# A transformer layer on eight cores: a second weight staging buffer, a reordered attention-output stage, and quantisation work moved between stages

## The reference

```python
# x: (8, 2048, 2048) fp32; Wq, Wk, Wv, Wo: (2048, 2048); w1: (8192, 2048); w2: (2048, 8192)
q, k, v = x @ Wq, x @ Wk, x @ Wv                       # per batch item, 2048 tokens
scores  = swapaxes(q) @ k / sqrt(64)                   # (feature, feature): 2048 x 2048
a       = swapaxes(softmax(scores, -1) @ swapaxes(v))  # contraction over features
x2      = layernorm(x + a @ Wo)
quant(w) = sign(w) * (abs(w) >= 0.7 * mean(abs(w)))    # whole-matrix mean
h       = gelu(x2 @ quant(w1).T + b1)
out     = layernorm(x2 + h @ quant(w2).T + b2)
```

## Time and profile before

| | us |
|---|---|
| median of two timed runs | 3946.72 (3915.34 and 3978.10) |
| the profiled execution | 3823.98 |
| its span on the slowest core (core 4) | 3822.4 |
| spans of the eight cores | 3772.3 to 3822.4 |
| TensorE busy | 3225.7 (84%) |
| VectorE busy | 1256.1 (33%) |
| ScalarE busy | 736.1 (19%) |

### The profile page before, as it was taken

One profiled execution on the slowest core, in us unless ns is written; L12 is line 12 of the kernel. 1 busy time (PEld: TensorE's weight loads), 2 busy tenths in 40 slices (PEclk: granted clock), 3 DMA queues, 4 the chain that ended last, 5 costly groups with the idle time before them and its releaser, 6 DMA issues. The chain is left out here.

```text
span 3822.4 us, 37269 instructions; the slowest of 8 cores (3772.3 to 3822.4 us)
## 1 busy us (share of the span) xinstructions
PE 3225.7 (84%) x14622; PEld 1459.4 (38%) x14917; DVE 1256.1 (33%) x1362; ACT 736.1 (19%) x1065; POOL 92.6 (2%) x166
## 2 busy tenths in 40 slices
PE   0997999935885887677669999999979999989997
PEld 0443444412332333233334444444434444434443
DVE  0111221102444444255533333443322333333333
ACT  1344513440111111233421111111110000300003
POOL 0000000000000000000000000000000000000000
PEclk9998999968997999888879999999989999989998
DMA  9899947974436444655557766777766223553232
GB/s 195 215 280 274 278 116 200 242 208 88 116 99 193 132 134 136 161 198 202 200 153 193 190 187 181 189 190 192 193 182 230 92 107 132 177 197 123 76 132 89
DMA packets 357615, 656.84 MB, mean 172 GB/s; under 512 B 177152, under 2 KB 234560, under 8 KB 332864
## 3 DMA queue, kind: packets, MB, share of 16 engines
q1 hardware_dynamic: 238704, 297.85, 25.5%
q0 software_dynamic: 41648, 184.60, 20.5%
q10 hardware_dynamic: 77088, 171.98, 13.7%
HBM read 536.98 MB, written 150.99 MB: 180 GB/s over the span
## 5 line engine op out<-in xcount | busy, mean ns | idle before, releaser
L920 PE MATMUL psH<-big,w1sl 128*128 128x512 bf16 x4014 | 885.2, 380 | 19.2 <-DMA w1sl<-w1q_h 14.2
L1014 PE MATMUL psF<-w2g,hg 128*128 128x512 bf16 x4012 | 887.0, 381 | 5.1 <-issue 0.8
L920 PEld LDWEIGHTS psH<-big,w1sl 128*128 128x128 bf16 x4096 | 399.6, 98 | 504.4 <-issue 29.4
L1014 PEld LDWEIGHTS psF<-w2g,hg 128*128 128x128 bf16 x4096 | 400.7, 98 | 491.3 <-issue 14.9
L1064 DVE TENSOR_TENSOR oacc<-psF,oacc 128x2048 f32<-128x2048 f32 x112 | 256.6, 2292 | 573.3 <-PE psF L1014 573.3
L229 DVE TENSOR_SCALAR qmask<-qin,tbc 128x1024 f32<-128x1024 f32 x256 | 208.0, 813 | 716.3 <-DMA qin<-w2t 456.1
L240 DVE TENSOR_TENSOR qout<-qmask 128x1024 bf16<-128x1024 f32 x256 | 313.7, 1225 | 168.8 <-DMA w2q_h<-qout 79.4
L436 ACT ACTIVATE qmask<-sbin 128x1024 f32<-128x1024 f32 x256 | 269.9, 1055 | 425.9 <-DMA sbin<-w1t 181.5
L303 PE MATMUL psA<-wbuf,big 128*128 128x512 bf16 x1004 | 228.4, 386 | 111.8 <-DMA wbuf<-wq 100.3
L656 PE MATMUL psO<-big,atsl 128*128 128x512 bf16 x1000 | 244.3, 407 | 83.6 <-ACT atsl L679 52.8
L937 ACT ACTIVATE hstg<-psH,b1sb 128x2048 bf16<-128x2048 f32 x64 | 125.9, 1967 | 753.7 <-PE psH L920 753.7
(11 more groups left out here) (107 smaller groups left out, 1094.5 us busy)
## 6 DMA issues: line engine op xcount, KB each, us to landing
qin<-w1t POOLq DMA_DIRECT2D x64, 1024.0 KB, 5.9
qin<-w2t POOLq DMA_DIRECT2D x64, 1024.0 KB, 7.4
w2g<-w2q_h SPq DMA_DIRECT2D x16, 4096.0 KB, 15.1
sbin<-w1t SPq DMA_DIRECT2D x64, 512.0 KB, 7.7
sbin<-w1t ACTq DMA_DIRECT2D x64, 512.0 KB, 7.5
sbin<-w2t SPq DMA_DIRECT2D x64, 512.0 KB, 7.4
sbin<-w2t ACTq DMA_DIRECT2D x64, 512.0 KB, 7.4
w1q_h<-qout SPq DMA_DIRECT2D x64, 512.0 KB, 7.1
```

The source lines that it names most:

```text
L920: mm = t.matmul(ps[:, nb * 512:nb * 512 + 512], w1sl[:, (f_m % 2) * 2048 + d_k * P: (f_m % 2) * 2048 + d_k * P + P], big0[:, d_k * S + nb ...
L1014: mm = t.matmul(ps[:, nb * 512:nb * 512 + 512], hg[:, slot * 8192 + f_k * 1024 + j * P: slot * 8192 + f_k * 1024 + j * P + P], w2g[:, slot ...
```

## The change

- QT_P2 goes from 24 to 32 tiles and QT_P3 from 56 to 64; p4 has 32 tiles left instead of 48. f1 is as it was.
- A second buffer qin2 takes the odd pairs. A pair's load now waits for the pair before the previous one. There are still two halves of one qout, under the same wait.
- In p2, POOL waits for the q and v stores before its first load, since qin2 lies where spillb was.
- In p3, atsl has two slots. TensorE transposes tiles 0 and 1 first and tile e_m + 2 after the matmuls of tile e_m; ScalarE copies tile e_m + 1 before it evacuates tile e_m. TensorE waits for v only once.
- In p4, VectorE first waits for all pair stores of p2 and p3.

```diff
-QT_P2 = 24
-QT_P3 = 56
+QT_P2 = 32
+QT_P3 = 64
@@ emit_quant_loads
                 for p in range(lo // 2, hi // 2):
-                    if p >= 1:
-                        g.wait_ge(g_qm.h, 2 * p)
-                    s_qin.issue(g, qin[:], w_pair_src(p))
+                    if p >= 2:
+                        g.wait_ge(g_qm.h, 2 * (p - 1))
+                    dst = qin if p % 2 == 0 else qin2
+                    s_qin.issue(g, dst[:], w_pair_src(p))
@@ emit_quant_vec
-                    src = qin[:, (i % 2) * 1024:(i % 2) * 1024 + 1024]
+                    qbuf = qin if (i // 2) % 2 == 0 else qin2
+                    src = qbuf[:, (i % 2) * 1024:(i % 2) * 1024 + 1024]
@@ p2, gpsimd
                                 g.wait_ge(g_bc.h, 1)
+                                c_q.wait_all(g)
+                                c_v.wait_all(g)
                                 emit_quant_loads(g, 0, QT_P2)
@@ p3
-                             nc.sbuf_tensor("atsl", [P, 2048], BF16) as atsl, \
+                             nc.sbuf_tensor("atsl", [P, 2 * 2048], BF16) as atsl, \
@@ p3, tensor
+                                trsp(0)
+                                trsp(1)
+                                for e_m in range(nE):
+                                    asl = atsl[:, (e_m % 2) * 2048:
+                                               (e_m % 2) * 2048 + 2048]
                                     t.wait_ge(a_trs.h, e_m + 1)
-                                    s_vre.wait_all(t)
+                                    if e_m == 0:
+                                        s_vre.wait_all(t)
                                     if e_m >= 1:
                                         t.wait_ge(a_oev.h, e_m)
...
+                                    if e_m + 2 < nE:
+                                        trsp(e_m + 2)
@@ p3, scalar
-                                    s.wait_ge(t_tr.h, e_m + 1)
-                                    if e_m >= 1:
-                                        s.wait_ge(t_o.h, e_m)
-                                    pt = psTA if e_m % 2 == 0 else psTB
-                                    s.copy(atsl[:], pt[:]).then_inc(a_trs.h, 1)
-                                    a_trs.inc(1)
+                                    if e_m == 0:
+                                        s.wait_ge(t_tr.h, 1)
+                                        s.copy(atsl[:, 0:2048],
+                                               psTA[:]).then_inc(a_trs.h, 1)
+                                        a_trs.inc(1)
+                                    if e_m + 1 < nE:
+                                        s.wait_ge(t_tr.h, e_m + 2)
+                                        if e_m >= 1:
+                                            s.wait_ge(t_o.h, e_m)
+                                        pt = psTA if (e_m + 1) % 2 == 0 else psTB
+                                        s.copy(atsl[:, ((e_m + 1) % 2) * 2048:
+                                                     ((e_m + 1) % 2) * 2048 + 2048],
+                                               pt[:]).then_inc(a_trs.h, 1)
+                                        a_trs.inc(1)
                                     s.wait_ge(t_o.h, e_m + 1)
-                                    s.wait_ge(t_tr.h, e_m + 1)
@@ p4, vector
+                            c_wq.wait_first_n(v, (QT_P2 + QT_P3) // 2)
```

More of the change, by code:

```diff
@@ L215, in emit_quant_loads @@
             def emit_quant_loads(g, lo, hi):
-                assert lo % 2 == 0 and hi % 2 == 0
                 for p in range(lo // 2, hi // 2):
-                    if p >= 1:
-                        g.wait_ge(g_qm.h, 2 * p)
-                    s_qin.issue(g, qin[:], w_pair_src(p))
+                    if p >= 2:
+                        g.wait_ge(g_qm.h, 2 * (p - 1))
+                    dst = qin if p % 2 == 0 else qin2
+                    s_qin.issue(g, dst[:], w_pair_src(p))
             def emit_quant_vec(v, lo, hi):
@@ L458, in _ @@
                         a_tcp.inc(1)
-                with nc.sbuf_tensor("qout", [P, 2 * 1024], BF16) as qout:
+                with nc.sbuf_tensor("qout", [P, 2 * 1024], BF16) as qout, \
+                     nc.sbuf_tensor("qin2a", [P, 2 * 1024], F32) as qin2:
                     if upto >= 2:
@@ L638, in _, with trsp @@
                                 g_id.wait_all(t)
-                                for e_m in range(nE):
+                                def trsp(e_m):
                                     pt = psTA if e_m % 2 == 0 else psTB
@@ L657, in _ @@
                                                 psO[:, sn * 512:sn * 512 + 512],
-                                                atsl[:, f_k * P:f_k * P + P],
+                                                asl[:, f_k * P:f_k * P + P],
                                                 big1[:, f_k * S + sn * 512:
@@ L687, in _ @@
                                     a_oev.inc(1)
-            with nc.sbuf_tensor("qout2", [P, 2 * 1024], BF16) as qout:
+            with nc.sbuf_tensor("qout2", [P, 2 * 1024], BF16) as qout, \
+                 nc.sbuf_tensor("qin2b", [P, 2 * 1024], F32) as qin2:
                 if upto >= 4:
```

## The result

The changed kernel took 3754.75 us in the median of its eleven runs, the kernel before 3825.72 us in the median of its ten. Some executions of either kernel, the two of before that were shown at first (3915.34 and 3978.10) among them, are over 1.5% above its fastest; without these, before lies between 3792 and 3832 us (six runs, mean 3808) and after between 3740 and 3778 (eight runs, mean 3754), a ratio of 0.9858 with a 95% interval of 0.9813 to 0.9902. The forecast ratio, 0.987, lies inside that interval, but the forecast time, 3897, is 3.8% above the measured 3754.75, and its whole range, 3775 to 3955, lies above it too. The profiled execution of before, 3823.98, is near the upper end of the six.

A forecast was written before the change was run, and what follows sets the result against it. TensorE was busy 84%, its recoverable idle time in p2, p3 and p4, held by waits; +12 +27 -80 -10 +2 = -49 us took 3824 to 3775, ratio 0.987, 3897 timed; own range 3856 to 3936, 8-in-10 range 3775 to 3955.

The forecast's parts named there:

- Part 1: p3: second qin buffer takes the load out of the chain, leaves the spill; pairs every 11.4 us, saving 0.2 each.
- Part 2: p3: 32 pairs instead of 28, and the stage cannot end before its last pair; +27 us, bounds +17 and +33.
- Part 3: p3: new TensorE order worth nothing since the pairs outlast it; without them 28 us and up to 25 of clock.
- Part 4: p2: with one pair per group, every group's qsl load waits behind a spill; +12 us, bounds 0 and +20.
- Part 5: p4: 16 pairs instead of 24, tiles every 16.2 us instead of 21.5; -80 us, and -10 in the tail.
- The two chains: p4: TensorE's own chain, 15.6 us a tile, and one spanning two tiles through VectorE and ScalarE, 15.7 a tile.
- B: p3: pairs run faster once the load is away; TensorE ends about 65 us earlier, 3829 us timed; chance 0.16.
- C: p4: transfers at 197 GB/s make a tile 18.6 us instead of 16.2; 36 us back, 3934 timed; chance 0.20.
- D: p3: the prefetch slows the spill, 31 intervals add 2.4 us each, 74 us; 3973 timed; chance 0.09.

The follow-up runs named there:

- later spill: Changed kernel with SyncE in p2 issuing a pair's spill after the next group's qsl load, not before it: ratio to before 0.9736.

## Why the prediction was right, and where it was wrong

**The step that failed is the last one, which took the median of two timed runs for the kernel's time.** "The median of the timed runs of before, 3946.72, stands 3.2% above the profiled execution; the ratio on it gives 3897." Two runs 1.6% apart were taken as the kernel's time, against a profiled execution below both. The later runs put before at 3825.72 in the median of ten, and at 3808 in the mean of the six behind the ratio: 0.987 of these is 3776 and 3758, where 3754.75 was measured. The sum on the profiled execution gave 3775, 0.5% above the measured median. The low end of the range, 3775, was the bare sum on the profiled execution with no room beneath it, although the prediction's best case was 88 us below its start.

**That the ratio came out right is in part luck.** The sum was -49 us. The stages give +23 (p2), +17 (p3), -98 (p4) and -4 (f1), with 3 us more ahead of p2: -59. The means of the runs differ by 54 us. But p2 was 14 us worse than forecast, and p3, p4 and f1 were 10, 8 and 6 us better.

**Part 1, the pair's pace: right.** The load's wait would be replaced by the spill's. It was (146.8 us), and the buffer alone left the pace at 11.2. The pace was taken as 11.4 and is 11.1, its lower bound: with one qin the load was the later of the two in most pairs and cost some 0.4 us more than the spill (11.5 against 11.1), where the term allowed 0.2.

**Part 2, p3: right in mechanism, +27 forecast, +17 measured.** The 10 us are the pace: 0.3 us over 31 intervals is 9.

**Part 3, the order: worth nothing, right.** TensorE would be done 50 us or more ahead; it idled for 81.8. Its tile takes 16.2 us where 16.7 was taken. Alone the order gave 11 us (p3's last evacuation no longer ends the block), and under two qout buffers, where nothing outlasts it, p3 follows TensorE. Its worth of 28 us "and up to 25 more of clock" came out at 57: the idle time before each tile fell from 3.7 to 3.9 us to 1.3, and the granted clock over the stage rose from 0.92 to 0.98.

**Part 4, p2: +12 forecast, +23 measured, and 3 more ahead of p2's first matmul.** The pattern and its size were right (32.5 to 34.2 us for two groups forecast, 34 measured in the first half). On core 4, whose rows the term was made from, p2's matmuls went from 255 us (first to last start) to 266: +11, inside the +4 to +15 forecast for the groups. But core 4 was the slowest in that stage; the median core had 246 and now has 267. The term was mis-sized because its base was one core. Two cores (0 and 1) need 280 to 282; the last section describes them, and the cause is open. The stretch from p2's last matmul to p3's first grew by 3 us as well (41 to 44). It is 44 to 47 us in the five kernels with the second qin and 40 to 42 in the four with one, so it goes with that buffer. The prediction had no term for it, and its reason was not looked for. The extra load at the start cost the 3 us that were forecast. This lies ahead of p2's first matmul, where the stage table does not see it: from the threshold's matmul to the first of the scores it was 12.7 us before and is 15.6 after (median of the cores). The row of before (core 4), to be read against the first row of p2 after:

```profile
924.99 43.48 PE L509 MATMUL psS<-big,qsl 128*128 128x512 bf16 x188 [12.10 <-DMA qsl<-q_h]
```

**Part 5, p4: -90 forecast, -98 measured.** The two chains were 15.6 and 15.7 us; 16.2 was taken with room for waits that did not come, and the tile takes 15.8: 6 us over 15 tiles. The tail's cast and evacuation end 15.9 us after the last matmul (1851.04 to 1866.94), 16.4 forecast. f1: +2 forecast, -4 measured; why it is shorter was not looked for.

**The rivals.** B, faster pairs: refuted for this change, and it is what happens with the second qout, where p3 loses the 73 us (65 forecast) that B had. The Trainium skill's advice ("Trainium Kernel Development and Optimization", section Best Practices) to double-buffer holds in the runs for the chain as a whole: one of two buffers doubled changed 11.5 us a pair to 11.1, both doubled made it 6.8. C, p4 held by transfers at 197 GB/s: refuted; p4 moved 209 GB/s and the tile still took 15.8 us. D, slower spills: refuted; the pairs come every 11.1 us, where D decides from 13.0.

## What to carry to other kernels

When a loop waits for a load and then, very shortly, for a store, the profile names one wait and hides the other beneath it. Before a buffer is doubled, measure from the end of the last work to the start of the next one against each condition by itself, and double the buffer of each condition that stands close behind. The second qout with a single qin was not run; by the earlier trace rows the spill added only 9.9 us over 27 pairs, so by this estimate it alone would have left the pace near 11.2 us (11.6 less 0.4). In a queue that issues both loads and stores, a store that waits for an engine holds up all loads behind it: put the load that is already free to go ahead of it. In the change as it was made the moved work paid most: the quotas alone gave 40 of the 62 us. And two timed runs, both above the profiled execution, are no base for a forecast in microseconds; a ratio can be right while the time is not.

## What the runs showed of the hardware that was not expected

Two transfers that seemed to need 6 to 7 us each side by side are no measure of the rate. In the changed kernel's p3 a load took 6.0 us and a spill 6.5 us to land (medians), and a pair's 1.5 MiB (1.57 MB) moved every 11.1 us, 142 GB/s. With two qout buffers they took 7.5 to 8.0 us each, and a pair moved every 6.8 us, 231 GB/s.

TensorE's granted clock fell in p2 on two of eight cores in a way that no gap explains. On core 1 two groups took 33.9 us after waits of 1.4 us, and 29.5 to 30.1 us after waits of 4.2 to 4.5. From 1049 to 1192 the granted clock of cores 0 and 1 was 0.81 and 0.80, that of the other six 0.89 to 0.92. Where the waits are gone (later spill), it does not occur. Why short waits cost two cores more than longer ones did is left open; no run told it apart. Nor does the length of a wait alone tell the clock behind it in p3: the last tile, after the same 2.21 us of idle time, took 13.97 us on core 1 of the changed kernel and 15.66 us on its core 6.
